# Gradient stage of a test-time-trained MLP: one silu tile per pair turned by a DMA instead of TensorE

## The reference

```
pred  = silu(k_flat @ w1.T + b1) @ w2.T + b2        # k_flat: 8*(64+1024) rows of 256, hidden 1024
loss  = 0.5 * sum((pred - v_flat) ** 2)
grads = grad(loss)((w1, b1, w2, b2))
upd   = (1 - alpha) * p - theta * g                  # for each of the four
```

## Time and profile before

| | |
|---|---|
| median of 3 runs | 2520.16 us (2519.02 to 2524.42) |
| the profiled execution | 2520.66 us |
| its span, first to last instruction | 2518.8 us |
| around the span | 1.9 us |
| gradient phase in the span | about 461.8 to 1469 us |
| PE busy | 2423.3 us, 96% |
| ACT, DVE, POOL busy | 1292.3, 1764.9, 1414.7 us |

### The profile page before, as it was taken

One profiled execution on the slowest core, in us unless ns is written; L12 is line 12 of the kernel. 1 busy time (PEld: TensorE's weight loads), 2 busy tenths in 40 slices (PEclk: granted clock), 3 DMA queues, 4 the chain that ended last, 5 costly groups with the idle time before them and its releaser, 6 DMA issues. The chain is left out here.

```text
span 2518.8 us, 41156 instructions
## 1 busy us (share of the span) xinstructions
PE 2423.3 (96%) x15649; PEld 2155.0 (86%) x15649; DVE 1764.9 (70%) x3704; ACT 1292.3 (51%) x2266; POOL 1414.7 (56%) x940
## 2 busy tenths in 40 slices
PE   6999999799999999999999989999999879999998
PEld 5888888688888888888888977777777769999998
DVE  6777776567766767767777676667666657777766
ACT  3787888544444444444444356555665524443333
POOL 2565666566666666666666634666666544333333
PEclk9999999999999999999999999999999979999999
DMA  3222222600000100100000132322221134444441
GB/s 123 71 91 70 92 67 84 250 28 26 26 26 26 32 28 26 30 26 26 26 26 22 53 95 76 102 95 92 91 85 58 33 126 134 139 142 136 153 135 57
DMA packets 135284, 190.33 MB, mean 76 GB/s; under 512 B 13426, under 2 KB 103959, under 8 KB 134960
## 3 DMA queue, kind: packets, MB, share of 16 engines
q1 hardware_dynamic: 121264, 157.27, 19.3%
q0 software_dynamic: 13824, 30.44, 3.6%
HBM read 123.13 MB, written 72.12 MB: 78 GB/s over the span
## 5 line engine op out<-in xcount | busy, mean ns | idle before, releaser
L2163 POOL TENSOR_TENSOR m_hl<-m_hf,m_hh 128x512 fp32r<-128x512 f32 x112 | 169.0, 1521 | 145.0 <-ACT m_hh L1826 144.9
L2524 POOL DMA_INDIRECT out<-e_ys,slot_token x80 | 83.1, 1039 | 231.4 <-DVE e_ys L2480 218.9
L104 PE MATMUL e_ps_y<-r_w_h,e_hl 128*128 128x256 f32 x640 | 181.2, 283 | 0.0
L104 PE MATMUL e_ps_y<-r_w_l,e_hh 128*128 128x256 f32 x640 | 179.0, 280 | 0.0
L104 PE MATMUL e_ps_y<-r_w_h,e_hh 128*128 128x256 f32 x640 | 178.9, 280 | 0.0
L824 POOL DMA_INDIRECT xbuf_d<-xn,scatter_rows x128 | 151.5, 1183 | 46.7 <-issue 38.1
L2413 ACT ACTIVATE e_hf<-e_ps_z,e_b 128x640 f32<-128x640 f32 x128 | 102.0, 797 | 146.8 <-PE e_ps_z L104 138.8
L681 POOL TENSOR_TENSOR prob<-prob,softmax_small 128x1024 f32<-128x1024 f32 x65 | 123.3, 1897 | 71.3 <-DVE softmax_small L616 71.3
L104 PE MATMUL e_ps_z<-slotsT_h,w_l 128*128 128x320 f32 x512 | 159.1, 311 | 1.0 <-DVE slotsT_l L2458 1.0
L104 PE MATMUL e_ps_z<-slotsT_l,w_h 128*128 128x320 f32 x512 | 159.0, 310 | 0.0
L104 PE MATMUL e_ps_z<-slotsT_h,w_h 128*128 128x320 f32 x512 | 158.8, 310 | 0.0
(11 more groups left out here) (313 smaller groups left out, 9077.4 us busy)
## 6 DMA issues: line engine op xcount, KB each, us to landing
shared_x<-in_x SPq DMA_DIRECT2D x32, 512.0 KB, 4.9
shared_xT<-xT_d SPq DMA_DIRECT2D x64, 256.0 KB, 4.6
new_w1T<-in_W SPq DMA_DIRECT2D x16, 1024.0 KB
new_w2T<-in_W SPq DMA_DIRECT2D x16, 1024.0 KB
xbuf_d<-new_w1T SPq DMA_DIRECT2D x16, 650.0 KB, 9.0
slots<-xbuf_d SPq DMA_DIRECT2D x15, 650.0 KB
xn_d<-xn SPq DMA_DIRECT2D x32, 256.0 KB, 2.5
xT_d<-shared_xT SPq DMA_DIRECT2D x32, 256.0 KB, 2.6
```

The costliest lines, as they stand in the source:

```text
L104: i = e.matmul(out, a, b, start=first and not onto and n == 0, stop=last and n == len(terms) - 1, skip_group_check=onto)
L2163: e.tensor_tensor(hl[:, t, 0:N], hf[(HC * C + t) % NZ][:, 0:N], hh[:, t, 0:N], ALU.subtract).then_inc(*h_low(C, t))
L2524: e.indirect_dma_start(io["out"], bass.IndirectOffsetOnAxis(ap=token[i % 2][:, b:b + 1], axis=0), ys[:, b], None, bounds_check=NT - 1, oob ...
```

## The change

The even tile of pairs 2 to 31, and the memory tile (pair 32), 31 tiles in all, no longer go through TensorE's transposes. In their place:

1. ACT copies `h_full`, seen as 2048 words of 16 bits in a row, into two planes of 1024 words (`split_words`), right after `h_h` of that tile. The planes lie in `shared.oT`.
2. SP issues one DMA with transpose of the 128 by 2048 words (512 KB) into `wordsT` (`move_words`).
3. ACT waits for it and joins the two planes back into fp32 words in `h_full`, 2048 words again (`join_words`), then rounds the two halves to hTh from there. The call stands in forward(p, 1), behind the first seed and ahead of the rounding of the odd tile's `h_full`.
4. POOL makes hTl of that tile in two halves (`rest_moved`), which DVE made before. POOL's list is put in another order: slope even, h_l even, dz_l even, slope odd, the two halves, dz_l odd, h_l odd, then both sums.
5. `predict` waits for the odd tile as before, and for each half of the even tile ahead of the matmuls that use it.

To make room, the second buffers of the slope's rest and of xn go. The load of xn for pair 1 moves behind the sixteen clearing DMAs, the load of xn(p+1) waits for `xn_low(p)`. In iteration 32 the DMA with transpose stands ahead of the loads of the old weights, and the last of these (now into `shared.oT`) waits until it has landed.

```diff
+def by_dma(p, b):
+    return p >= 2 and b == 0
...
-        out += [("hT", g, i) for i in range(2) if now]
+        out += [("hT", g, i) for i in range(2) if now and not by_dma(p, 0)]
...
-        rest = [sb("silu_rest", [P, HID]), shared.oT]
+        rest = sb("silu_rest", [P, HID])
+        words = shared.oT[:].bitcast(U16).rearrange("p (s n) -> p s n", s=2)
+        wordsT = sb("h_wordsT", [P, 2 * HC, P], U16)
...
-        xn_f = [sb(f"xn_f{i}", [P, 2, D]) for i in range(2)]
+        xn_f = sb("xn_f", [P, 2, D])
...
             def predict(p):
-                pe.wait_ge(*hT_low.at(2 * p + blocks_of(p) - 1, 1))
+                if p < NPAIR:
+                    pe.wait_ge(*hT_low.at(2 * p + 1, 1))
...
+                    for half in range(2):
+                        ks = range(4 * half, 4 * half + 4)
+                        if by_dma(p, 0):
+                            pe.wait_ge(*moved_low.at(2 * p, half))
...
+            def split_words(g):
+                act.wait_ge(*words_moved.at(moved_before(g)))
+                e.activation(words, hf[g % 2][:].bitcast(U16).rearrange("p (n s) -> p s n", s=2), ACTF.Copy).then_inc(*words_made(g))
+
+            def join_words(g):
+                act.wait_ge(*words_moved.at(g))
+                act.wait_ge(*h_low.at(g))
+                act.wait_ge(*pred_done.at(g // 2 - 1))
+                e.activation(hf[g % 2][:].bitcast(U16).rearrange("p (n s) -> p s n", s=2),
+                             wordsT[:].rearrange("p (s k) t -> p s (k t)", s=2), ACTF.Copy).then_inc(*words_joined(g))
+                act.wait_ge(*words_joined.at(g))
+                for half, hc in enumerate(cols):
+                    ks = slice(4 * half, 4 * half + 4)
+                    e.activation(hTh[:, ks, block[g % 2]], hf[g % 2][:, hc].rearrange("p (k t) -> p k t", k=4), ACTF.Copy).then_inc(*moved_high(g, half))
...
                 seed(2 * g + ZBANKS)
+                if b and by_dma(p, 0):
+                    join_words(g - 1)
                 act.wait_ge(*h_half.at(g, 1))
                 act.wait_ge(*g2_done.at(p - 2, 3))
                 e.activation(hh[g % 4][:], hf[g % 2][:], ACTF.Copy).then_inc(*h_high(g))
+                if by_dma(p, b):
+                    split_words(g)
                 seed(2 * g + ZBANKS + 1)
...
+            def rest_moved(g):
+                for half, hc in enumerate(cols):
+                    ks = slice(4 * half, 4 * half + 4)
+                    pool.wait_ge(*moved_high.at(g, half))
+                    e.tensor_tensor(hTl[:, ks, block[g % 2]], hf[g % 2][:, hc].rearrange("p (k t) -> p k t", k=4),
+                                    hTh[:, ks, block[g % 2]], ALU.subtract).then_inc(*moved_low(g, half))
...
+                rest_dz(g - 2)
+                if 2 <= p < NPAIR:
+                    slope(g + 1)
+                if by_dma(p, 0):
+                    rest_moved(g)
+                rest_dz(g - 1)
+                if 2 <= p < NPAIR:
+                    rest_h(g + 1)
+                sum_dz(g - 2)
+                sum_dz(g - 1)
...
+            def load_xn(p):
+                n = blocks_of(p)
+                sp_.wait_ge(*xn_low.at(p - 1))
+                e.dma_start(xn_f[:, 0:n], io["xn_d"][p][:, 0:n]).then_inc(*xn_in(p))
+
+            def move_words(g):
+                if moved_before(g) < 0:
+                    sp_.wait_ge(*oT_out.at(NGRP - 1, 1))
+                sp_.wait_ge(*words_made.at(g))
+                sp_.wait_ge(*words_joined.at(moved_before(g)))
+                e.dma_start(wordsT[:], words.rearrange("p s n -> p (s n)"), transpose=True).then_inc(*words_moved(g))
...
             e.dma_start(b1c[:], io["b1c"]).then_inc(*b1c_in(0))
+            load_xn(1)
             for p in range(PAIRS + 1):
+                for b in range(2):
+                    if p < PAIRS and b < blocks_of(p) and by_dma(p, b):
+                        move_words(2 * p + b)
```

More of the change, by code:

```diff
@@ L848, in gradient_banks @@
         out += [("g2", p - 1, 0)] if old else []
-        out += [("hT", g, i) for i in range(2) if now]
+        out += [("hT", g, i) for i in range(2) if now and not by_dma(p, 0)]
         out += [("g2", p - 1, 1)] if old else []
-        out += [("hT", g + 1, i) for i in range(2) if both]
+        out += [("hT", g + 1, i) for i in range(2) if both and not by_dma(p, 1)]
         out += [("g2", p - 1, t) for t in (2, 3) if old]
@@ L951, in gradient_phase @@
             signal(n, [0], 16) for n in ("g_ident_in", "g_scale_in", "g_b2_in", "g_rates_in", "g_b1c_in"))
-        xT_in, xn_in, oT_in = ([signal(f"g_{n}_in{i}", [p for p in pairs if p % 2 == i and (p or n != "xT")], 16)
-                                for i in range(2)] for n in ("xT", "xn", "oT"))
+        xT_in, oT_in = ([signal(f"g_{n}_in{i}", [p for p in pairs if p % 2 == i and (p or n != "xT")], 16)
+                         for i in range(2)] for n in ("xT", "oT"))
+        xn_in = signal("g_xn_in", pairs, 16)
         rows_out = signal("rows_out", range(SLOTS // P // CLEAR), 16)
@@ L963, in gradient_phase @@
         h_half, rest_made = signal("h_half", kinds["z"]), signal("rest_made", kinds["z"])
+        moved_tiles = [2 * p + b for p in pairs for b in range(blocks_of(p)) if by_dma(p, b)]
+        words_made, words_moved = signal("words_made", moved_tiles), signal("words_moved", moved_tiles, 16)
+        words_joined = signal("words_joined", moved_tiles)
+        moved_high, moved_low = (signal(n, [(g, half) for g in moved_tiles for half in range(2)]) for n in ("moved_high", "moved_low"))
         hT_low, dz_half = signal("hT_low", kinds["hT"]), signal("dz_half", kinds["dh"])
@@ L998, in freed, with h_taken, moved_before @@
                     "g2": g2_added, "g1": g1_added}[kind].at(*key)
+        def h_taken(g):
+            return moved_low.at(g, 1) if by_dma(g // 2, g % 2) else hT_done.at(g, 1)
+        def moved_before(g):
+            n = moved_tiles.index(g)
+            return moved_tiles[n - 1] if n else -1
         def xT_ready(p):
@@ L1004, in gradient_phase @@
         old += [(g2[:, 4 * k:4 * k + 4], w2T_v[:, 4 * k:4 * k + 4]) for k in range(2)]
-        old_sb = [t[:] if n < 2 else t[:].rearrange("p (a b) -> p a b", b=D) for n, t in enumerate([sp[1], rest[1], hf[1], rest[0]])]
+        old_sb = [t[:] if n < 2 else t[:].rearrange("p (a b) -> p a b", b=D) for n, t in enumerate([sp[1], hf[1], rest, shared.oT])]
         def tensor(e):
@@ L1034, in predict @@
                     mc = slice(m * P, (m + 1) * P)
-                    i = matmul_split(e, acc[:, m * 2 * P:m * 2 * P + N], [(w2Th[:, k, mc], w2Tl[:, k, mc]) for k in range(HC)],
-                                     [(hTh[:, k, 0:N], hTl[:, k, 0:N]) for k in range(HC)])
+                    for half in range(2):
+                        ks = range(4 * half, 4 * half + 4)
+                        if by_dma(p, 0):
+                            pe.wait_ge(*moved_low.at(2 * p, half))
+                        i = matmul_split(e, acc[:, m * 2 * P:m * 2 * P + N], [(w2Th[:, k, mc], w2Tl[:, k, mc]) for k in ks],
+                                         [(hTh[:, k, 0:N], hTl[:, k, 0:N]) for k in ks], first=half == 0, last=half == 1)
                 i.then_inc(*pred_done(p))
@@ L1099, in tensor @@
                     accumulate_w2(p - 1, 0)
-                if now:
+                if now and not by_dma(p, 0):
                     transpose_h(p, 0)
@@ L1103, in tensor @@
                     accumulate_w2(p - 1, 1)
-                if both:
+                if both and not by_dma(p, 1):
                     transpose_h(p, 1)
@@ L1233, in scalar @@
                     backward(p - 1, 1)
-                if now:
+                if p == NPAIR:
+                    join_words(2 * p)
+                elif now and not by_dma(p, 0):
                     round_hT(p, 0)
@@ L1410, in vector @@
                 add_w2(p - 1, 0)
-                rest_hT(p, 0)
+                if not by_dma(p, 0):
+                    rest_hT(p, 0)
                 add_w2(p - 1, 1)
@@ L1537, in sync @@
                     sp_.wait_ge(*slope_made.at(TILES - 1))
+                    e.dma_start(old_sb[2], old[2][1]).then_inc(*old_in[2](0))
+                    sp_.wait_ge(*words_moved.at(TILES - 1))
                     e.dma_start(old_sb[3], old[3][1]).then_inc(*old_in[3](0))
```

59 lines of the change are left out of this document (28 added, 31 removed).

## The result

The changed kernel takes 2575.85 us (median of 4 runs, 2573.23 to 2576.85), the kernel before 2522.29 us beside it: a ratio of 1.0224 [1.0211, 1.0236], so 2.2% slower. One of the four executions of the kernel before was slow (2866.81 us); the ratio leaves it out, the median of 2522.29 doesn't. The profiled executions have spans of 2571.4 and 2518.8 us, 52.6 us apart, at a mean granted clock of 0.979 and 0.986. The forecast was 2561 us, 40 us more than before. It came out 15 us higher, inside the range and inside the likeliest case's own range.

A forecast was written before the change was run, and what follows sets the result against it. PE, busy for all of the loop, was taken to bound the kernel. 30 pairs at 1.2 us (2.05 waited less 0.87 saved) give 35 us, head 3, tail 2: 40 on 2520.66, so 2561 us, range 2499 to 2735.

The forecast's parts named there:

- the likeliest case: In each full pair, passes of 1.92 us and a DMA of 3.9 to 6 us: 2531 to 2594 us, chance 0.50.
- What goes, 0.87 us a tile: PE ahead of predict: without one tile's eight transposes predict could begin 0.87 us sooner, 27 us over 31 tiles.
- How late ACT becomes: ACT's list ahead of predict: two passes of 1.92 us make the pair 0.1 us longer even without waiting for the DMA.
- The bound for a stride that costs a second access: ACT's split and join: upper bound of double the 1.92 us for a pass, if the stride of two costs twice.
- The DMA: Transposing DMA ahead of the join: 4.9 us from issue to landing, so predict waits 2.05 us, pair 1.2 us longer.
- the rival with a wait of 6.1 us: Crowded DMA of 9.0 us in each pair, with 1.7 us lost to half clock: 2734 us, chance 0.17.
- POOL, DVE's slack, the room made: Among the pairs: POOL's two halves of 1.2 us each and DVE's later steps stay hidden behind other work.
- Head and tail: Once each: later xn load in the head, 3 us; memory tile and late old weights in the tail, 2 us.
- A short 16-bit pass: ACT's split and join: a pass costs 1.06 us, all 27 us kept less 5, 2499 us, chance 0.13.
- A DMA under 3.9 us: In each pair, passes of 1.92 us and a quicker DMA: about 2529 us, down to 2520, chance 0.12.
- the blocks aren't paid one after another: Opposite of a rival: sixteen DMA blocks paid one by one, 20 to 32 us, over 3060 us, chance 0.08.
- The even case: Nearly even pairs, 0.1 us longer each, with a DMA under 3.9 us: about 2529 us, chance 0.12.

The follow-up runs named there:

- The first experiment: Changed kernel with the rounding of the odd tile's transposes placed right behind the join and the even tile's roundings in ACT's list: 2506.07 us, ratio 0.9941.
- the last pair of kernels: Two kernels with xn of pair 1 loaded earlier, against the kernel before: no tile by DMA, 2516.19 us; reordered ACT list and thirty tiles by DMA, 2491.22 us.
- the new head: Reordered kernel with the memory tile back on TensorE, plus xn of pair 0 split sooner and xn of pair 1 loaded among the clearing DMAs: 2493.71 us.
- the half join: Changed kernel with the join writing only the plane of high words, 1024 in place of 2048: 2528.05 us, ratio 1.0036.

## Why the prediction was right, and where its sizes were off

- **What goes, 0.87 us a tile.** Right. The first experiment's pair is 0.86 us shorter, and the last pair of kernels gives 0.83 a tile.
- **How late ACT becomes.** The chain held link for link. Seed to sigmoid is 1045.40 - 1043.34 = 2.06 us, as in the earlier trace rows, and the join's earliest start is what the working gave, 5.9 us behind the split's. Of its terms the split was right (1.92 taken, 1.90 measured), and the join was too small: 1.92 taken, 2.59 measured. The bound for a stride that costs a second access stood beside it, but no rival had its price, and I applied one value to both passes; the stride costs only where it is written. The Trainium skill (ScalarE: Activation LUTs, What ACT_TABLE_LOAD costs) gives 0.833 ns an element for fp32 and bf16 alike, by which a pass is an estimated 1.89 us. The trace agrees for the split, 1.90, and for the join without a stride, 1.91; it doesn't for the join as it is, 2.59.
- **The DMA.** Taken at 4.9 us from the plain row with the same bytes, it landed in 4.3. The join starts 1046.29 - 1040.07 = 6.22 us behind the split where the sum had 6.95, some 0.7 too late, and ACT waits 0.29 us for the landing and not 1. This and the join's missing 0.67 nearly cancel, which is luck: the usual pair is 1.07 us longer where the sum had 1.2, so what PE loses to the wait is 1.07 + 0.87 = 1.94 us, where the sum had 2.05. (The profile's 1.70 counts from the modelled end of the matmul before.)
- **What was missed: the clock in the likeliest case.** I priced half clock for the rival with a wait of 6.1 us and left it out at 2 us, as if a wait of that size were free. Nine of 30 pairs had such a stretch, 14 us; with 4 us of longer waits this is the term that the 40 us lacked in the pairs, and another 10.2 us at half clock stand in the tail. No row of before showed PE after a wait of 2 us in this loop, and the sum should have carried an end for it.
- **POOL, DVE's slack, the room made.** Hidden, as costed: PE never waits for POOL's halves among the pairs, and the kernel without the move is even with before. In the memory tile PE does wait 1.94 us for them, since no odd tile covers POOL there.
- **Head and tail.** The sum of the two is near, its parts aren't: 3 and 2 us taken, 1.1 and 6.2 measured in this trace. The head's own cost isn't steady: `predict` of pair 0 to that of pair 1 takes 28.65 to 30.53 us (27.52 before) in the eight traces that load xn as the changed kernel does (all but those of before and of the new head), so 3 was its upper end.

In the head, ACT's, DVE's and PE's views of the changed kernel have these rows:

```profile
500.49 0.63 ACT L1166 ACTIVATE xn_h<-xn_f 128x512 fp32r<-128x512 f32 x1 [4.32 <-DMA xn_f<-xn_d]
```

```profile
496.20 1.59 DVE L1312 TENSOR_TENSOR xn_l<-xn_f,xn_h 128x512 fp32r<-128x512 f32 x1 [1.44 <-ACT xn_h L1166]
...
501.76 0.68 DVE L1377 TENSOR_TENSOR shared_x<-g_bank,shared_x 128x512 f32<-128x512 f32 x1
```

```profile
PE g_bank L1047 <- DVE shared_x L1377: 4.8, 1, 4.8
```

ACT waits 4.32 us for xn of pair 1, and DVE and PE wait behind it, as forecast. But the load that frees PE starts earlier than I had it: DVE's `xn_low(0)` takes 1.59 us and ends at 497.8, and not at 499.9, which I had read out of the merged row. So the data land at 500.4 in place of 502.6, and PE's wait grows from 3.52 us to 4.8, not by the 3 us of the sum. In the tail the last fold starts only once ACT has scaled the last old weights, at 1499.10, as forecast; that alone would put the residual 1.4 us further behind `predict` than before (1502.2 - 1494.42 against 1449.20 - 1442.87). It starts another 1.5 us later because PE's own `predict` runs at half clock, and so do the steps behind it up to 1505.9 (`w_l`, +1.9). The sum had only the late `predict` and the late fold; what it left out is again the clock behind a wait of 1.94 us.

**The rivals.** A short 16-bit pass is out: no pass took 1.06 us, and the half join alone took 1.40. A DMA under 3.9 us and one of 9.0 are out at 4.3 (5.6 at most). The Trainium skill (VectorE: DVE Perf Modes, The three transpose paths) has 1309 ns for one block of 128 by 128; sixteen of them in one DMA took 4.3 us in all and not 21, so the blocks aren't paid one after another. The even case, ACT behind by no more than PE gains, is what the half join shows, at 0.50 us of wait. Which part of ACT's 0.3 us wait for the DMA is SP's own time in the issue was not tried.

## What to carry to other kernels

Work taken off a full engine is a gain only if what it leaves behind is not late on another one; ask for the last link ahead of the first matmul that waits, and not for the other engine's share of busy time. When ACT, DVE and POOL work through written-out lists, place the instruction that TensorE waits for as early in the list as its operands allow: here one call placed three instructions earlier turned 2.2% slower into 0.6% faster, and with head and tail put right into 1.1 to 1.2%. A wait of TensorE of 2 us is to be priced above its own length, since the clock fell behind nine of thirty of them here.

## What the runs showed of the hardware that I had not expected

- **A write with a stride of two words of 16 bits costs ACT a third more.** 2048 words take 2.59 us written with the stride, 1.91 in a row, and 1.90 when the stride is on the reading side; 1024 words written with it take 1.40 us.
- **A transposing DMA of 512 KB is as quick to land as a plain one** (4.3 us against 4.8 to 4.9), although it holds SP for longer: 1.3 to 3.1 us, median 1.85, for each instruction, where the loads of xn and oT have a median of 0.32. It has many more packets: the packets of queue 1 go from 121264 to 185744, which is 64480 / 31 = 2080 for each, all of them under 512 bytes (13426 such packets before, 77907 after).
- **The clock after short waits.** Among the pairs, no stretch at half clock followed PE's waits of usually 0.5 us (half join; at most 1.4), 1.0 us (join in a row; at most 1.9) and 1.3 us (no wait for the DMA). In the changed kernel, with waits of 1.2 to 3.0 us, 9 of 30 pairs had one, and with waits of 3.0 to 4.5 us (one more pass) all of them. Which pairs are hit near 1.7 us stays open, and length doesn't decide it: `predict` at 699.86 had waited 1.72 us and was hit, the one at 1054.35 had waited 1.70 and was not, nor was the one at 1023.04 with 2.34. In the memory tile a wait of 0.8 us (half join) had 10.2 us at half clock behind it.
